# Token stacks split once, scores of 512 columns, unread products, block-diagonal biases, smaller groups and paired spreads in a four-block network

## What is computed

```python
q = (x @ Wq).reshape(b, t, h, k).transpose(0, 2, 1, 3) * scale      # 8 heads of 64, 8 images of 256 tokens
kk = (x @ Wk).reshape(b, t, h, k).transpose(0, 2, 1, 3) * scale
attn = jax.nn.softmax(jnp.einsum('bhqk,bhsk->bhqs', q, kk), axis=-1)
out = jnp.einsum('bhqs,bhsk->bhqk', attn, v)                        # then @ Wu + bu
```

## Time and profile before

| what | value |
|---|---|
| median of 3 runs | 392.93 us (392.71 to 396.93) |
| the profiled execution | 395.99 us, span of its trace 394.2 us |
| mean granted TensorE clock of it | 0.918 |
| PE busy | 349.9 us (89%) |
| DVE, ACT, POOL busy | 271.4, 211.5, 161.5 us |
| HBM | 29.73 MB read, 0.72 MB written |

### The profile page before, as it was taken

How to read it: one execution, slowest core, us unless ns; L and a number is a source line. 1 busy time by engine, 2 the same in 40 slices (tenths; PEclk the granted TensorE clock), 3 DMA queues, 4 the chain that set the end, 5 groups by cost and what they waited for, 6 DMA issues and landing times. The chain is left out here.

```text
span 394.2 us, 7158 instructions
## 1 busy us (share of the span) xinstructions
PE 349.9 (89%) x2458; PEld 240.1 (61%) x2461; DVE 271.4 (69%) x661; ACT 211.5 (54%) x523; POOL 161.5 (41%) x171
## 2 busy tenths in 40 slices
PE   8885489999999999999769999858377899999996
PEld 5642367888888888887454233436065666666662
DVE  2988867888888888877472854786884645555541
ACT  2455458777767776777428344360324444444440
POOL 5000325545555455545200000050100399999995
PEclk9996569999999999999968999975588999999999
DMA  8942000000000000000001990000001856665531
GB/s 214 246 153 65 0 1 2 2 0 3 0 2 2 2 2 0 2 1 2 2 0 44 341 357 15 0 0 2 0 2 38 296 178 216 198 199 194 192 109 53
DMA packets 16436, 30.92 MB, mean 78 GB/s; under 512 B 5968, under 2 KB 9744, under 8 KB 16400
## 3 DMA queue, kind: packets, MB, share of 16 engines
q1 hardware_dynamic: 15936, 29.64, 23.4%
q10 hardware_dynamic: 464, 0.82, 1.0%
HBM read 29.73 MB, written 0.72 MB: 77 GB/s over the span
## 5 line engine op out<-in xcount | busy, mean ns | idle before, releaser
L513 POOL TENSOR_TENSOR va_vb<-va_vb,rowinv 128x512 f32<-128x512 f32 x64 | 66.5, 1040 | 70.4 <-DVE rowinv L1677 70.4
L633 ACT ACTIVATE va_vb<-ps,negmax 128x256 f32<-128x256 f32 x128 | 59.8, 477 | 8.0 <-DVE negmax L1670 7.8
L766 ACT ACTIVATE wy<-ps 128x512 f32<-128x512 f32 x64 | 38.1, 597 | 47.1 <-PE ps L1101 47.1
L1101 PE MATMUL ps<-XP,early 64*128 64x256 f32 x512 | 58.0, 380 | 1.5 <-DVE hid_g L1738 1.5
L1101 PEld LDWEIGHTS ps<-XP,early 64*128 64x128 f32 x512 | 46.6, 186 | 14.8 <-issue 5.5
L1670 DVE TENSOR_REDUCE negmax<-ps 128x2 f32<-128x512 f32 x64 | 44.1, 688 | 8.2 <-PE ps L902 8.0
L902 PE MATMUL ps<-keys_gates,xcur 128*128 128x256 f32 x256 | 48.0, 311 | 1.4 <-DVE keys_gates L1662 1.4
L902 PEld LDWEIGHTS ps<-keys_gates,xcur 128*128 128x128 f32 x256 | 35.6, 195 | 13.9 <-issue 11.3
L913 PE MATMUL ps<-consts,va_vb 128*128 128x128 f32 x256 | 39.1, 275 | 2.8 <-POOL va_vb L513 2.3
L929 PE MATMUL ps<-pT,vproj 128*64 128x256 f32 x256 | 34.5, 392 | 0.0
L913 PEld LDWEIGHTS ps<-consts,va_vb 128*128 128x128 f32 x256 | 30.2, 148 | 6.8 <-POOL va_vb L513 4.2
(11 more groups left out here) (323 smaller groups left out, 700.6 us busy)
## 6 DMA issues: line engine op xcount, KB each, us to landing
pT<-gates_row SPq DMA_DIRECT2D x16, 512.0 KB, 5.1
vproj<-gates_row SPq DMA_DIRECT2D x14, 512.0 KB, 4.8
gate_row_keys<-gates_row SPq DMA_DIRECT2D x14, 512.0 KB, 5.0
early<-in_f_in SPq DMA_DIRECT2D x1, 2048.0 KB, 8.2
consts<-in_consts SPq DMA_DIRECT2D x1, 816.0 KB, 7.3
x<-in_x SPq DMA_DIRECT2D x1, 512.0 KB, 3.7
w2raw<-in_f_in SPq DMA_DIRECT2D x1, 512.0 KB, 5.3
out<-in_f_out SPq DMA_DIRECT2D x1, 512.0 KB
```

What stands on the lines that cost most here:

```text
L513: gp.tensor_tensor(prob[:, n % 4], prob[:, n % 4], rowinv[:, n % 4, :].unsqueeze(2).broadcast_to([P, U, N]), ALU.mult).then_inc(S("p_scale ...
L633: ins = act.activation(prob[:, n % 4, u, :], ps[:, 1 + n % 2, u * N:(u + 1) * N], ACT.Exp, bias=negmax[:, n % 4, u:u + 1], accum_out=rowsu ...
L766: act.activation(act_out[:, kk % 2, :].rearrange("p (o n) -> p o n", o=2), ps[:, 2 * pair_of(kk):2 * pair_of(kk) + 2, 0:2 * P], ACT.Silu). ...
L1101: mm = pe.matmul(ps[:, 2 * pair_of(kk) + o, w * 2 * P:(w + 1) * 2 * P], w3raw[r, e, w * HID:(w + 1) * HID], pairs(c, 2)[r], start=True, st ...
```

## The change

It has five parts.

1. *First attention.* `XS` and `xcur` give way to `XX`, which holds high and low tokens apart, each in both 64-row halves. Seven parts of tokens are split straight out of the transposes, by ACT (`token_high`) and DVE (`token_low`), 64 rows each, and POOL copies five of them to the other 64 rows (`double_tokens`); the first image is transposed into two banks and needs none. The weights are `AA` and `GG`, high on 64 rows and low on the others. The keys of a pair need two products, not four; they go to `Z`, high keys of a head on its own rows and low ones on the other head's, in two copies on ACT and two on DVE of 64 rows. A tile of scores is now one query tile of two heads instead of two query tiles of one, by two products of 512 columns. DVE starts the pseudo-inverse ahead of the norm.
2. *Unread products* at four more places.
3. *Biases* of FFN 2: `b2two` is block-diagonal, two products of the full array, no wait.
4. *Groups* of 4 in FFN 2, FFN 3 stays at 8.
5. *Spreads* two chunks at a time, from different 64-row halves (`spread_two`).

```diff
-RING, GROUP = 16, 8
+RING, GROUP2, GROUP3 = 16, 4, 8
...
-        XS = sb("XS", [P, TILES * P], F32R)
+        XX = sb("XX", [P, 2, G, J * N], F32R)
...
+        AA = sb("AA", [P, HEADS, C], F32R)
+        GG = sb("GG", [P, HEADS * C], F32R)
...
-            return kk % 2 if kk < CHUNKS else (kk - 2) % 3
+            return kk % 2 if kk < CHUNKS else (kk - 4) % 3
...
+            def double_tokens(i):
+                g, j, count, o, _, _ = TOKEN_PARTS[i]
+                at = slice(j * N, (j + count) * N)
+                gp.wait_ge(S("x_low"), i + 1)
+                gp.tensor_copy(XX[rows_of(1 - o), :, g, at],
+                               XX[rows_of(o), :, g, at].bitcast(F32)).then_inc(S("x_doubled"), 1)
...
-                act.activation(KH[:, k % 2].rearrange("p h n -> p (h n)"), ps[:, 0, :],
-                               ACT.Copy).then_inc(S("kh_ready"), 1)
+                for h in range(2):
+                    act.activation(Z[rows_of(h), q % 2, h, :], ps[rows_of(h), 0, 0:N],
+                                   ACT.Copy).then_inc(S("kh_ready"), 1)
...
-                    pe.matmul(o, AH[:, head].rearrange("p d c -> p (d c)"), xcur[:, g, :], start=True, stop=False)
-                    mm = pe.matmul(o, AL[:, head].rearrange("p d c -> p (d c)"), xcur[:, g, :],
-                                   start=False, stop=True)
+                for part in range(2):
+                    mm = pe.matmul(ps[:, 0, 0:N], AA[:, 2 * pair:2 * pair + 2, :].rearrange("p h c -> p (h c)"),
+                                   tokens(part, m), start=(part == 0), stop=(part == 1))
...
-                for u in range(U):
-                    for part, K in enumerate((KH, KL)):
-                        mm = pe.matmul(ps[:, 1 + n % 2, u * N:(u + 1) * N], xcur[:, g, u * P:(u + 1) * P],
-                                       K[:, k % 2, n % 2, :], start=(part == 0), stop=(part == 1))
+                for part in range(2):
+                    mm = pe.matmul(ps[:, 1 + u, :], tile_of(part, q // 4, u),
+                                   Z[:, q % 2].rearrange("p h n -> p (h n)"), start=(part == 0), stop=(part == 1))
...
+            pe.wait_ge(S("gT_ready"), 2 * n + 2)
             if c >= 2:
-                pe.wait_ge(S(weighed), c - 1)
+                pe.wait_ge(S(weighed), c)
             if n == 0:
+                for o in range(2):
+                    pe.matmul(ps[:, spread_bank(c + o), :], first_row[rows_of(o), o, :],
+                              gT[rows_of(o), 2 * c:2 * c + 4, :], start=True, stop=True).then_inc(S("gates_spread"), 1)
             else:
+                for turn in range(2):
+                    for d in range(2):
+                        o = (d + turn) % 2
+                        mm = pe.matmul(by_parity(ps[:, spread_bank(c + d), :])[:, o], first_row[rows_of(o), o, :],
+                                       gT[rows_of(o), 2 * (c + d):2 * (c + d) + 2, :], start=True, stop=True)
+                        mm.then_inc(S(("half_spread", "gates_spread")[turn]), 1)
+                    if turn == 0:
+                        pe.wait_ge(S("half_spread"), c + 2)
...
+                for half in range(2):
+                    pe.matmul(ps[:, 6 + half, :], b2two[:], gT[:, 4 * half:4 * half + 4, :],
+                              start=False, stop=False, skip_group_check=True)
...
-                if kk == CHUNKS:
+                if kk == CHUNKS + 2:
                     pe.wait_ge(S("f3_hid_ready"), CHUNKS)
...
+            pe.wait_ge(S("logits_taken"), 4)
+            keep_clock(pe, 4, 8)
             gates_pe(pe, 1)
...
+            pe.wait_ge(S("v3_ready"), 1)
+            keep_clock(pe, 5, 8)
             pe.wait_ge(S("v3_ready"), 2)
...
+            keep_clock(pe, 5, 8)
             pe.wait_ge(S("rotated"), 4)
...
+            keep_clock(pe, 2, 12)
             ln_pe(pe, 1)
```

More of the change, by code:

```diff
@@ L665, in attention_act, with step @@
-            attention_steps(act, step)
+            def step(q):
+                if there(q + 2):
+                    key_high(q + 2)
+                if q < 0:
+                    token_high(act, 2 * q + 7)
+                    token_high(act, 2 * q + 8)
+                if there(q + 1):
+                    exponentials(2 * q + 2)
+                if there(q):
+                    transposed_copy(act, 2 * q)
+                if q % 4 == 3 and there(q + 1):
+                    value_copy((q + 1) // 4, 0)
+                if q % 4 == 0 and there(q):
+                    value_copy(q // 4, 1)
+                if there(q + 1):
+                    exponentials(2 * q + 3)
+                if q % 4 == 0 and q >= 4:
+                    out_copy(q // 4 - 1)
@@ L667, in _ @@
+            attention_steps(step)
         @block.scalar
@@ new lines, in value, with scores @@
+            def value(m, u):
+                if u == 0:
+                    upto(pe, "stream_added", m - 1)
+                await_image(pe, m)
+                upto(pe, "v_ready", U * m + u)
+                for part in range(2):
+                    mm = pe.matmul(ps[:, 7, :], tile_of(part, m, u), GG[:], start=(part == 0), stop=(part == 1))
+                mm.then_inc(S("v_projected"), 1)
+            def scores(n):
+                q, u = n // 2, n % 2
+                pe.wait_ge(S("k_ready"), 2 * q + 2)
+                upto(pe, "probs_ready", n - 1)
+                for part in range(2):
+                    mm = pe.matmul(ps[:, 1 + u, :], tile_of(part, q // 4, u),
+                                   Z[:, q % 2].rearrange("p h n -> p (h n)"), start=(part == 0), stop=(part == 1))
+                mm.then_inc(S("scores_ready"), 1)
@@ new lines, in turn, with products @@
+            def turn(n):
+                pe.wait_ge(S("p_scaled"), n + 1)
+                upto(pe, ("pT_even", "pT_odd")[n % 2], n // 2)
+                for h in range(2):
+                    for su in range(U):
+                        at = (U * h + su) * P
+                        mm = pe.transpose(ps[:, 3 + n % 2, at:at + P], prob[:, n % 4, h, su * P:(su + 1) * P], ident)
+                mm.then_inc(S("p_turned"), 1)
+            def products(q):
+                m = q // 4
+                pe.wait_ge(S("pT_even"), q + 1)
+                pe.wait_ge(S("pT_odd"), q + 1)
+                pe.wait_ge(S("v_ready"), U * (m + 1))
+                if q == 0:
+                    pe.wait_ge(S("x_low"), len(TOKEN_PARTS))
+                if q % 4 == 0:
+                    upto(pe, "outT_ready", m)
@@ L993, in attention_pe, with step @@
-            pe.wait_ge(S("fold_split"), 3)
-            pe.sem_inc(S("pv_done"), PAIRS)
-            pe.sem_inc(S("out_turned"), G)
-            attention_steps(pe, step)
+            def step(q):
+                i = q - 2
+                if there(q + 1):
+                    scores(2 * q + 2)
+                if newton_in(q):
+                    pe.wait_ge(S("nsx_ready"), i + 2)
+                if there(q + 2):
+                    keys(q + 2)
+                if newton_in(q):
+                    newton_a()
+                if q == 0:
+                    pe.wait_ge(S("x_low"), 5)
+                if there(q):
+                    turn(2 * q)
+                if there(q + 1):
+                    scores(2 * q + 3)
+                if q % 4 == 3 and there(q + 1):
+                    value((q + 1) // 4, 0)
+                if q % 4 == 0 and there(q):
+                    value(q // 4, 1)
+                if q % 4 == 1 and q >= 5:
+                    turn_out(q // 4 - 1)
+                if newton_in(q):
+                    pe.wait_ge(S("nsy_ready"), i + 1)
+                if there(q):
+                    turn(2 * q + 1)
+                if newton_in(q):
+                    newton_b()
+                if there(q - 1):
+                    products(q - 1)
@@ L1055, in ffn2_pe @@
             gates_pe(pe, 0)
-            for c in range(CHUNKS):
-                if c % 2 == 0:
-                    for kk in range(4 + 2 * c, 8 + 2 * c):
-                        hidden(kk)
-                spread(pe, 0, c, "f2_hid_ready")
+            for c in range(0, CHUNKS, 2):
+                for kk in range(4 + 2 * c, 8 + 2 * c):
+                    hidden(kk)
+                spread_two(pe, 0, c, "f2_hid_ready")
             for kk in range(12, RING):
@@ L1653, in while_first_keys @@
[L1653 to L1669 removed]
+            layer_norm(0)
```

469 lines of the change are left out of this document (191 added, 278 removed).

## The result

The changed kernel took 381.85 us (381.27 to 382.36, 4 runs) where the kernel before took 393.55 (392.71 to 396.93): a ratio of 0.9687, 95% interval 0.9653 to 0.9721. It is 11.7 us faster, against 19.4 forecast, and lies just above the range of 367.5 to 381. Over all runs, 14 of the changed kernel have a mean of 381.8 and 55 of the one before 394.0: 12.2 us.

The account below looks back on a forecast made before the run. TensorE (PE) was taken to bound the kernel. Terms of 0.5 + 1.0 + 5.4 + 0.6 + 5.6 + 1.5 + 0.5 + 4.3 = 19.4 us, off the 392.93 median, gave 373.5 us (forecast 371 to 377, range 367.5 to 381).

Parts of the forecast that it names:

- The 24 pairs: First attention, pairs with a pseudo-inverse step: two key products fewer save PE 0.23 us a pair, taken as 5.4 us.
- spreads: First FFN: spreading two chunks' gates from alternating 64-row halves, which run beside each other, saves 1.9 us.
- biases: First FFN: two full products replace four quarter-size ones run one after another, 2.0 us saved.
- groups: First FFN: hidden products in groups of four instead of eight wait less for activations, 1.7 us saved.
- The start of FFN 2: Second norm to first outputs: 1.9 us from spreads plus 1.5 from a burst of twelve unread products keeping the clock up.
- The base: Starting time for the sum: the 19.4 us gain was taken off the median of 392.93, giving 373.5 us.
- The start of the attention: Up to the fifth pair's keys: 0.5 us from merged low weights, net 1.0 from dropping the stack copy, less doublings.
- The last eight pairs: End of the first attention, at the ACT-DVE loop except where PE also computes values: 0.6 us gained, at most 1.9.
- The second attention: Two bursts of eight unread products around the value sums: +2 with clock up, -3 to 0 with it down; +0.5 us taken.
- The last FFN's start: First two chunks spread together at full clock, hidden products by 304.8 us: 4.3 us gained, POOL may cost up to 1.
- rival (b): Clock not held and a burst in the way: 2.0 us lost and 3.4 for the cold burst, 379 us; chance 0.14.
- (e): Rival for the whole kernel: two of the named losses happen together, 382 to 388 us; chance 0.06.

Follow-up runs that it names:

- the kernel with the new attention alone: The changed kernel without added bursts, with old biases, groups of eight and single full-row spreads; 386.94 us, ratio 0.9831 to the kernel before.
- the second trace of before: The kernel before, unchanged, profiled once more: 394.41 us median of 10 runs, the profiled one 394.07, span 392.3.
- the kernel with the later splits: The changed kernel with splits of token parts 5 and 6 behind ACT's first exponentials and DVE's second maxima; 381.23 us, ratio 0.9684.

## Why the prediction was wrong

*Right, with the size.* The 24 pairs: 5.4 forecast, 5.0 measured from first traces and from second ones, by the mechanism named (keys, PE-bound). The parts of FFN 2: spreads 1.9 and 1.8, biases 2.0 and 1.9, groups 1.7 and 1.55. The start of FFN 2 in all, 3.4 and 2.9 to 3.5, but that agreement is in part luck: its burst gave 0.5 of the 1.5 forecast, and 0.6 of the 3.5 is the first profile's longer half clock. Another 0.4 shows in the kernel with the new attention alone, which has neither (18.01 against 18.38). POOL in the last FFN: it starts 2.6 us behind the fifth hidden chunk, now on its gate row, and finishes in time; nothing lost.

*The base.* "It lies 3 us above the median of 392.93, from which 19.4 gives 373.5": the terms were read from the profiled execution, 2.4 us above the median of 393.55, and I took all 19.4 off the median, although 1.7 us of that execution's time in cold stretches (first pairs, FFN 2) was gone in the next one, at 394.07. I had seen the 3 us and not asked where they lay. Between the second traces of both kernels, 392.3 and 380.6, the difference is the 11.7 of the medians.

*The start of the attention* (1.0 and 0.5 forecast, 0 measured, -1.0 against the second trace of before). That -1.0 is not the order's doing alone: before's second trace had 3.4 us of half clock between the first and the fifth pair's keys, the other three of the table 8.5 to 11.0. With 8.5 before and 9.0 now, the pairs took 16.11 and 16.23. The low halves of the weights are one operation instead of two, but, in the mean of three traces with the old attention and eight with the new, the operation behind it came only 0.4 us earlier and ACT's first token copy 0.3, which the pseudo-inverse's earlier start takes. The stack copy's 1.31 us gave 0.2: norm to first keys went from 3.80 to 3.61, and the first scores stand at 50.85 where I expected 49.3. I charged the splits to DVE and the doublings to POOL; the wait ended with ACT, whose splits stand in front of the first exponential. The doublings were cheap: 0.6 us for 64 x 512 elements, and 1.03 for 64 x 1024, where I feared 1 to 2.

*The last eight pairs* (0.6 forecast, -0.4 measured). I took the halves at 0.33 us each from a copy over 128 rows of the same width, 0.66 for two, which is what two such halves took in the kernel before; two of 64 rows took 0.78 on ACT and 0.87 on DVE. And I had them 0.23 us earlier and hidden: the exponential that is queued behind them came 0.18 later. The saving on PE was there (0.46); what the rest of the new order costs, 0.83, had no term.

*The second attention* (+0.5 forecast, +0.8 and -0.9 measured). The cost of the burst at half clock was in the text, at 3.4 us. What failed is "what hides the second burst is the wait for DVE's rotation": the first burst delays the value sums so far that the second one no longer fits in front of it. In seven traces with both bursts besides these two the stretch is 34.9 to 37.2, in those without 34.2 to 35.7.

*The last FFN's start* (4.3 forecast, 2.1 to 2.4 measured). From first spread to fifth hidden chunk it is 4.3 us, half a microsecond better than worked out. The step that failed is "Afterwards: clock up", and what lies in front of the spreads with it. In before's trace the clock was full from 289.1, 2.5 us ahead of this norm. In the changed kernel's three it stayed half until 7 us behind the norm, so transposes, logits and hidden products ran cold (0.75 us, as in the kernel without bursts), and the burst came on top (1.2): 2.0 us. That was rival (b), named for the two other bursts and not for this one. Three other traces with all four bursts show the forecast's own condition, among them the kernel with the later splits, whose clock was full from 278.1:

```profile
279.69:292.91 13.22, 11.62 (x135) 7.96 (x138) 9.51 (x34) 5.66 (x9) 0.00 (x0) 1.00 0.09 16
```

There norm to fifth hidden chunk is 13.2 us, 4.3 less than before. So the sum of this stretch was right for a full clock, and no row told whether the changed list would find the clock full. The spreads' wait for both gate copies, 0.4 us, is in it.

By size, short of the forecast: base 1.7, start of the attention 1.8 to 2.2, the last FFN's start 1.9 to 2.2, last pairs 1.0, 24 pairs 0.4; the second attention from 0.3 better to 1.4 worse. They overlap, as the start of the pairs is in the first two. Rival (b) gave 379 and the two losses together 382 to 388; I had given (e) 0.06 as if losses were independent, though three of my terms leaned on the same clock.

## What to carry to other kernels

Before a profile's stretch is a term in a sum, ask for it in a second execution: here PE- and DVE-bound stretches repeated within 0.2 us and those with half clock in them moved by up to 2.2. A burst of unread products was free here only where the engine would have waited for longer than the burst lasted; at half clock it lasted too long, joined the path, and gave back what it won elsewhere. Before adding one, compare its length at half clock with the wait, and ask whether what follows needs the same slack. A split of an operation over engines has to be placed by the list of each: count what stands in front of the first instruction that someone waits for.

## What was new about the hardware

The places where the clock falls and returns shift between executions of one program: in three traces of the changed kernel the first half clock ended at 54.3, 59.1 and 54.1 us, with 3.4 us more of it behind in the first and third, and the long one at 286.4, 287.8 and 286.2. Over the traces with the new attention a long cold stretch of over 27 us began at 249.3 to 262.2 us; in five of fifteen the half clock came in shorter pieces instead. An ACT copy of 256 columns out of PSUM took 0.38 us, over 64 rows and over 128 alike. Two in a row took 0.78 when each had its own 64 rows, and 0.66 when both had all 128; one of 512 columns over 128 rows took 0.60. DVE's two subtractions took 0.87 and 0.76 in the same places. Spreading products in one 64-row half ran beside hidden products of the other in FFN 2, so that the rows of L1061 and L1083 interleave from 208.98 to 210.32 us in the changed kernel's trace.
